# Causal mask of a second attention: from mask products on TensorE to selects on GpSimd

## The reference

```python
h = _rms(x, n1_w)                       # x: 4 x 256 x 128
q = _rms(heads(wq), qn_w); k = _rms(heads(wk), kn_w); v = heads(wv)   # 16 heads of width 8
scores = jnp.einsum('bhqd,bhkd->bhqk', q, k) * HD ** (-0.5)
causal = jnp.tril(jnp.ones((T, T), bool))
scores = jnp.where(causal[None, None], scores, -jnp.inf)
attn = jax.nn.softmax(scores, axis=-1)
ao = jnp.einsum('bhqk,bhkd->bhqd', attn, v).transpose(0, 2, 1, 3).reshape(B, T, C) @ wo.T
ao = ao.at[:, :, :M].set(0.0)           # M = 32
x = x + ao
xf = _rms(x, n2_w).reshape(-1, C)       # then four experts with top-2 gating
```

## Time and profile before

| | |
|---|---|
| three runs | 288.17, 284.63, 287.77 us; median 287.77 |
| the profiled execution | 285.92 us; its span 284.2 us |
| granted TensorE clock, mean | 0.971 |
| PE, DVE, ACT, POOL busy | 77%, 57%, 45%, 26% of the span |

### The profile page before, as it was taken

How to read it: one execution, slowest core, us unless ns; L and a number is a source line. 1 busy time by engine, 2 the same in 40 slices (tenths; PEclk the granted TensorE clock), 3 DMA queues, 4 the chain that set the end, 5 groups by cost and what they waited for, 6 DMA issues and landing times.

```text
span 284.2 us, 4855 instructions
## 1 busy us (share of the span) xinstructions
PE 219.1 (77%) x1906; PEld 150.6 (53%) x1906; DVE 160.8 (57%) x335; ACT 128.5 (45%) x175; POOL 74.1 (26%) x77
## 2 busy tenths in 40 slices
PE   0387987788988899885924697878985997788983
PEld 0244454424444644642724484556663885777973
DVE  1888699372552682582474878858515145842313
ACT  0206695882744254250350427976576340524230
POOL 4516589910005026039006022000003011000000
PEclk9999999999999999997995899999999999999997
DMA  6800090000052060150060000000000000000000
GB/s 199 374 1 0 7 287 11 0 1 2 0 128 42 25 145 0 41 127 2 18 144 7 0 0 2 0 2 0 1 2 0 2 0 0 1 21 18 0 18 18
DMA packets 10067, 11.73 MB, mean 41 GB/s; under 512 B 928, under 2 KB 9648, under 8 KB 9792
## 3 DMA queue, kind: packets, MB, share of 16 engines
q1 hardware_dynamic: 10048, 11.47, 14.3%
HBM read 10.38 MB, written 1.09 MB: 40 GB/s over the span
## 4 chain that ended last, share of the span: by engine, by line
PE 53%; DVE 25%; ACT 11%; POOL 4%; issue 4%; DMA 2%; POOLq 0%; DVEq 0%; SPq 0%; ACTq 0%
PE banks L1516 11%; PE banks L1272 8%; PE banks L1239 5%; DVE probs L888 5%; PE banks L1300 4%; PE banks L1551 3%; PE banks L1167 3%; PE banks L1421 3%; PE banks L1371 2%; ACT probs L546 2%; PE banks L1292 2%; DMA rows<-in_rows 2%; PE banks L1399 2%; PE banks L1322 2%; ACT probs L585 2%
## 5 line engine op out<-in xcount | busy, mean ns | idle before, releaser
L888 DVE TENSOR_TENSOR probs<-probs,eb 128x1024 f32<-128x1024 f32 x24 | 29.7, 1251 | 31.9 <-ACT probs L546 31.9
L585 ACT ACTIVATE probs<-banks,shift 128x1024 f32<-128x1024 f32 x24 | 26.4, 1116 | 24.6 <-PE banks L1403 24.6
L1272 PE MATMUL banks<-probs,kvt 128*64 128x512 f32 (+1 forms) x128 | 24.9, 522 | 8.5 <-DVE probs L888 8.3
L546 ACT ACTIVATE probs<-banks,key_shift 128x1024 f32<-128x1024 f32 x24 | 25.9, 1112 | 12.0 <-PE banks L1239 11.5
L1239 PE MATMUL banks<-qt,kT 64*128 64x512 f32 x96 | 25.3, 628 | 2.6 <-ACT probs L546 2.1
L360 POOL TENSOR_TENSOR qin<-qss,minus_half 128x16 f32<-128x16 f32 x8 | 23.1, 2904 | 7.9 <-DVE qss L727 7.7
L1272 PEld LDWEIGHTS banks<-probs,kvt 128*64 128x64 f32 x128 | 8.2, 144 | 22.1 <-DVE probs L888 12.2
L1371 PE MATMUL banks<-ident_bf,parts 128*128 128x128 bf16 x128 | 10.1, 242 | 11.8 <-DVE parts L961 9.3
L1117 DVE SCALAR_TENSOR_TENSOR x<-banks,ga,x 128x96 f32 (+1 forms) x32 | 10.2, 318 | 15.4 <-PE banks L1551 11.4
L1167 PE MATMUL banks<-wa,on 128*128 128x512 f32 x32 | 17.3, 667 | 1.2 <-DVE spread L733 1.2
L389 POOL TENSOR_TENSOR o_raw<-o_raw,spread 128x2048 f32<-128x2048 f32 x2 | 9.1, 4540 | 30.4 <-DMA spread<-softmax_inverse_sums 30.4
(11 more groups left out here) (214 smaller groups left out, 442.3 us busy)
## 6 DMA issues: line engine op xcount, KB each, us to landing
spread<-softmax_inverse_sums SPq DMA_DIRECT2D x16, 256.0 KB, 5.9
eb<-bias_table SPq DMA_DIRECT2D x4, 512.0 KB, 6.2
wb<-in_wb SPq DMA_DIRECT2D x1, 1842.0 KB, 10.9
wa<-in_wa SPq DMA_DIRECT2D x1, 1160.0 KB, 7.4
x<-in_x SPq DMA_DIRECT2D x1, 512.0 KB, 4.1
softmax_inverse_sums<-zin SPq DMA_DIRECT2D x4, 128.0 KB, 1.7
out<-x SPq DMA_DIRECT2D x4, 128.0 KB, 1.8
rows<-in_rows SPq DMA_DIRECT2D x1, 456.0 KB, 6.0
```

What stands on the lines that cost most here:

```text
L546: nc_.activation(pb[c], sc[:, 1024 * (c % 2):1024 * (c % 2 + 1)], ACT.Exp, bias=key_shift[:, b, k:k + 1]).then_inc(s["exp_done"], 1)
L585: nc_.activation(pb[c], sc[:, 1024 * SLOT[c]:1024 * (SLOT[c] + 1)], ACT.Exp, bias=shift2[:, 3:4]).then_inc(s["exp2_done"], 1)
L888: v.tensor_tensor(p, p, w, ALU.mult).then_inc(s["mult_done"], 1)
L1272: last = mm(out, vn[:, b, part], rhs, start=(part == 0), stop=(part == 2))
```

## The change

The tiles `later` and `later_bf` go, with the POOL instructions that build them, and the 48 mask products (two in each of 24 chunks). Each score product now stands alone in its region of PSUM. POOL gets an `affine_select` for each chunk, which writes zeros over the exponentials of later keys, in place: four blocks of 128 columns for chunks with k < 2 (512 elements in a partition), eight for k = 2 (1024). Each waits for the chunk's exponential. `values2` waits for the selects of its group instead of for the exponentials. POOL's order in the first batch is written out: selects 0 to 2 ahead of `rstd_of_y(2)`, select 3 behind it, selects 4 and 5 between `rstd_of_y(3)` and `group_rstd(2)`. For the later batches POOL's hardware loop becomes a Python loop, with the copy into `v2f` and then the six selects; the roots of the second norm come behind the last of them.

```diff
--- before.py
+++ after.py
@@ -109,7 +109,6 @@
 
         ident = sb("ident", [P, P])
         sum_rows = sb("sum_rows", [P, 4, 32])
-        later = sb("later", [P, P])
         minus_half = sb("minus_half", [P, H])
         ln_eps = sb("ln_eps", [P, B * T])
         rms_eps = sb("rms_eps", [P, 4])
@@ -192,7 +191,6 @@
         rest = sb("rest", [P, 3, T * H, HD])
         v2 = qt[:, 0].rearrange("p m i -> p (m i)")[:, B * S:2 * B * S].rearrange("p (b t h d) -> p b t h d", b=B, t=T, h=H)
         ident_bf = sb("ident_bf", [P, P], BF16)
-        later_bf = sb("later_bf", [P, P], BF16)
         gain2 = sb("gain2", [P, HD])
         v2f = sb("v2f", [P, T, H, 32])
         o2s = keys_space[:, B * S:B * S + 1024].rearrange("p (g c) -> p g c", g=2)
@@ -239,7 +237,7 @@
             zmax_done zinv_ready zinv_stored zinv_spread on_ready y_done y_parts y_stat y_var y_rstd y_norm x2_done
             r_stat r_var r_rstd h2_ready h2_turned hT2_ready qkv_done raw_ready sq2_ready s64_ready r64_ready qkn_ready
             v2_done sq_x_ready p3_dve
-            v2f_ready operands_zeroed part_done parts_ready parts_turned operands2_ready qk2_chunk exp2_done pv2_done o2_evac o2_turned ao_ready ao_turned
+            v2f_ready operands_zeroed part_done parts_ready parts_turned operands2_ready qk2_chunk exp2_done later_zeroed pv2_done o2_evac o2_turned ao_ready ao_turned
             aoT_ready wo_done x3_done p4_dve
             f_stat f_var f_rstd f_ready f_turned xfT_ready gate_done lg_ready gate_w xs_ready gates
             gate_exp res_part u_done u_act silu_a h1_ready down_done stored""".split()
@@ -332,7 +330,7 @@
 
             pool.iota(pos[:], pattern=[[P, T]], base=0, channel_multiplier=1,
                       allow_small_or_imprecise_dtypes=True).then_inc(s["pos_ready"], 1)
-            for buf, value in ((minus_half, -0.5), (ln_eps, 1e-5), (ident, 0.0), (later, 0.0), (sum_rows, 0.0),
+            for buf, value in ((minus_half, -0.5), (ln_eps, 1e-5), (ident, 0.0), (sum_rows, 0.0),
                                (tri, 1.0), (rms_eps, EPS * D)):
                 pool.memset(buf[:], value)
             pool.memset(xk[:, :, P - 1:P], 0.0)
@@ -340,8 +338,6 @@
             step(pool.memset(kvs[:, :, KEYS:XS], 0.0))
             pool.affine_select(out=ident[:], in_=ident[:], compare_op=ALU.not_equal, fill=1.0, base=0,
                                pattern=[[-1, P]], channel_multiplier=1)
-            pool.affine_select(out=later[:], in_=later[:], compare_op=ALU.is_ge, fill=-FAR, base=0,
-                               pattern=[[1, P]], channel_multiplier=-1)
             for k in range(4):
                 pool.memset(sum_rows[:, k, k:k + 1], 1.0)
             pool.affine_select(out=tri[:], in_=tri[:], compare_op=ALU.is_ge, fill=0.0, base=-1,
@@ -392,7 +388,6 @@
                 rstd(mv[:, :, 1], ln_eps, ve[:], rs[:], s["y_stat"], s["y_rstd"], s["y_var"], b)
 
             pool.tensor_copy(ident_bf[:], ident[:])
-            pool.tensor_copy(later_bf[:], later[:])
             pool.memset(v2f[:], 0.0)
             pool.memset(parts[:], 0.0).then_inc(s["sums_cleared"], 1)
             normalised(0)
@@ -408,6 +403,13 @@
                 pool.wait_ge(s["pv2_done"], 2 * b)
                 pool.tensor_copy(v2f[:, :, :, 0:HD], v2[:, b]).then_inc(s["v2f_ready"], 1)
 
+            def later_zeros(b, c):
+                pool.wait_ge(s["exp2_done"], 6 * b + c + 1)
+                n = 4 if c % 3 < 2 else 8
+                block = pb[c].rearrange("p (n i) -> p n i", n=n)[:, :, 0:P]
+                pool.affine_select(out=block, in_=block, compare_op=ALU.is_ge, fill=0.0, base=0,
+                                   pattern=[[0, n], [1, P]], channel_multiplier=-1).then_inc(s["later_zeroed"], 1)
+
             group_rstd(0)
 
             pool.wait_ge(s["qk_chunk"], 6 * (B - 1))
@@ -416,13 +418,20 @@
             normalised(B - 1)
             pool.wait_ge(s["v2_done"], 1)
             values2_in_place(0)
+            for c in range(3):
+                later_zeros(0, c)
             rstd_of_y(B - 2)
+            later_zeros(0, 3)
             group_rstd(1)
             rstd_of_y(B - 1)
+            later_zeros(0, 4)
+            later_zeros(0, 5)
             group_rstd(2)
             pool.wait_ge(s["v2_done"], 3)
-            with pool.Fori(1, B) as b:
+            for b in range(1, B):
                 values2_in_place(b)
+                for c in range(6):
+                    later_zeros(b, c)
 
 
             for h in range(2):
@@ -1396,16 +1405,11 @@
                         lhs, rhs = kT2[:, e, m, 0:P], qT2[:, m]
                     else:
                         lhs, rhs = kT2[:, e, m, P:S], qT2[:, m, P:S]
-                    mm(sc[:, at + wide * i:at + wide * (i + 1)], lhs, rhs, start=(i % (n // 2) == 0), stop=False, skip_group_check=True)
-
-                for j in range(2):
-                    bank = halves(sc[:, at + 512 * j:at + 512 * (j + 1)], n // 2)
-                    last = mm(bank[:, :, 0:P], ident_bf[:], later_bf[:, None, :].to_broadcast([P, n // 2, P]), start=False, stop=True,
-                              skip_group_check=True)
+                    last = mm(sc[:, at + wide * i:at + wide * (i + 1)], lhs, rhs, start=True, stop=True)
                 last.then_inc(s["qk2_chunk"], 1)
 
             def values2(b, g):
-                pe.wait_ge(s["exp2_done"], 6 * b + 3 * g + 3)
+                pe.wait_ge(s["later_zeroed"], 6 * b + 3 * g + 3)
                 pe.wait_ge(s["v2f_ready"], b + 1)
                 pe.wait_ge(s["p4_dve"], 1)
                 if not (isinstance(b, int) and b == 0):
```

## The result

The changed kernel takes 298.7 us (median of five, 295.3 to 301.1) against 287.8 us (median of five, 284.5 to 288.2 and one of 563.9): the ratio is 1.037, with a 95% interval of 1.031 to 1.044. I had forecast 290.9, with 297.0 as the upper end. The profiled execution took 298.68 us, its span 297.0 us, 12.8 us more than before.

A forecast was written before the change was run, and what follows sets the result against it. It took the kernel as mostly PE-bound (53% of the chain). The walk's +2.5 us and 0.6 for DVE's company made +3.1: 285.92 became 289.0, plus 1.85 to the runs' median gave 290.9 us, range 286.5 to 297.0.

The forecast's parts named there:

- walk of waits: Second attention, batch by batch to the second norm's roots: select waits less mask gains, +2.5 us.
- the 0.6 that I had added: Addition to the walk: four of six selects run beside DVE's copies or splits, 0.15 us more each.
- DVE's company: POOL is slower beside DVE: 0.15 us more on four of six selects, +0.6 us in all.
- Rival 2: PE's clock halves in the last batch's idle gaps, slowing gate and first expert's products: up to 2 us, 292.9; chance 0.10.
- the 3.92 us of the earlier trace: Idle time before 131.07 us, after which the granted clock stood at half; each new single gap is shorter.
- The 2.9 us: Most that removing the mask products can give: eleven places on the chain, nine short pairs and two long.
- three signs: Prediction wrong if select's mean is over 1.5 or under 0.5 us, first batch comes later, or last batch's clock falls.
- upper end of 297.0: Top of the forecast range for the whole kernel, set to take in most of rival 1.
- rival 1: Six selects on the path run at the two-operand rate, 2.27 us each: 9.9 us slower, 297.7 us; chance 0.17.
- the select's price: POOL's select costs what a copy would: 1.04 us for eight blocks, about 0.61 us for four.
- POOL's order: First norm's root not delayed by selects; second norm's roots queue behind the last select and start 2.53 us later.

The follow-up runs named there:

- e2: Neither mask products nor selects, against the kernel before; values wait for the exponentials: 290.2 us, ratio 1.010.
- e1: Changed kernel with the 48 mask products put back, selects and the values' wait for them kept: 296.3 us, 1.035 times the kernel before.
- e3: Kernel before's mask products kept; POOL runs same-shaped selects on a spare stretch and values don't wait for them: 292.8 to 298.1 us over four runs.
- e4: Changed kernel with four or eight identity products on PE ahead of each wait for the selects: 298.2 us, 1.041 times the kernel before.
- e7: Changed kernel with batch 0 masked by products on PE, batches 1 to 3 by POOL's selects: 292.4 us, 1.021 times the kernel before.

## Why the prediction was wrong

*The walk of waits was right.* Distances between the landmarks of my walk, before, forecast and measured, in us; (1,0) is the values product of batch 1, group 0, and the last column takes off what the values product between them took over 1.51 us:

| from, to | before | forecast change | measured change | less slow values |
|---|---|---|---|---|
| values (1,0) to (1,1) | 4.90 | +0.88 | +2.43 | +1.15 |
| (1,1) to (2,0) | 7.29 | -0.61 | -0.70 | -0.70 |
| (2,0) to (2,1) | 4.90 | +0.89 | +1.01 | +1.01 |
| (2,1) to (3,0) | 6.71 | -0.03 | +1.29 | +0.23 |
| (3,0) to the roots | 4.41 | +1.40 | +1.41 | +1.41 |
| sum | 28.21 | +2.53 | +5.44 | +3.10 |

(Starts before: 187.67, 192.57, 199.86, 204.76, 211.47 and 215.88; after: 191.66, 198.99, 205.58, 211.49, 219.49, 225.31. Values (1,0) took 2.79 us, (2,1) 2.57. The starts before are the chain's, by which I had walked; the timeline has 187.60, 199.79 and 211.40 for three of them, and by it the sums are +5.37 and +3.03.) The waits came to 3.1 us, my 2.5 and the 0.6 that I had added; that this 0.6 was DVE's company is not borne out, since the six selects on the path took 1.09 us each with DVE beside some of them. That the roots stand behind the last select was right.

*Rival 2 was the step that failed, in its chance and in its price.* I gave the clock 0.10 and up to 2 us, in one place, the last batch, wrote against it that each single gap is shorter than the 3.92 us of the earlier trace rows, and forecast everything behind the gate at its old length. The runs show that this was no bound. In the changed kernel PE finished its scores of the first batch at 158.80 and the mean of the microsecond from 160 to 161 was already 0.79:

```profile
160.00:161.00 1.00, 0.00 (x0) 0.00 (x0) 1.00 (x3) 0.51 (x1) 0.78 (x2) 0.79 0.00 0
...
161.00:162.00 1.00, 0.00 (x0) 0.00 (x0) 1.00 (x1) 0.00 (x0) 0.91 (x1) 0.50 0.00 0
```

The row PEclk of the page shows how often it came: six separate groups of slices under 9, where before there were two and the last slice. Its price in this profile: about 3 us of PE's work in the first stretch (transposes, values, one projection at 2.4 us instead of 1.53), 2.3 us in the two values products of the table, and 3.0 us after the gate: some 8.3 of 12.8 us. With 3.1 for the waits, 1.8 for DVE (below) and 1.1 less at the start, 0.7 us are left. About 0.4 of it lies between the roots and the gate (3.63 us, 3.23 before), which waited for the last values at half clock; the rest is the wait for a select ahead of the values at 191.66 (0.56 us), where my walk had the select and the mask's gain cancel. In whole runs: the kernel before itself took 285.0 us at a mean clock of 0.970 and 287.4 at 0.952, and without selects or products (e2) it went to 290.2 at 0.935. I had also looked only at the wait that the change adds. e2 has no new wait and loses 1%, at lower levels of the clock in eight of ten runs: there the mask products were work that kept the clock up, at no cost on most of the path. They are not all of it: e1 and e3 have all of them, and their clock is 0.938 and 0.937. The 2.9 us that I set as the most their removal can give was right as a bound and said nothing about the loss.

The Trainium skill (TensorE: Matmul & The Clock Gate, Part 1), which I had named for this rival, says that the gate looks at recent activity. e2's levels and e4's last batch, whose values behind their filler take 1.51 us instead of 2.79, agree with it. I used it for one place and one gap.

*The price of DVE's company was put on the wrong engine.* This is the second step that failed. I charged POOL 0.15 us for running beside DVE. What happened is that DVE ran slower beside POOL: 5.15 us for a split of 3.37, shown by e3 (no wait, same length) and e7 (no select, 3.38). The row was there: beside the slowed copy of the earlier trace rows, at 194.30, the kernel before has a slowed cast of DVE, and I read the pair for POOL alone:

```profile
159.12 0.55 DVE L947 CAST parts<-qt 128x768 bf16<-128x768 f32 x1
...
194.55 0.76 DVE L947 CAST parts<-qt 128x768 bf16<-128x768 f32 x1
```

In the first batch I had walked only POOL's queue, which did hold (the root at 163.82 waited for DVE, not for a select), and not the engine beside it, which PE waits for. This is +1.8 us. It isn't what made the clock fall there: the fall came at about 160.6, and an undisturbed split would have ended at 161.1.

*My signs and my range.* Two of the three signs that I had named for a wrong prediction came: the first batch came out later (its values at 165.59, against 163.85, although its split began 1.1 us earlier), and the clock fell in the last batch; the gate came 9.8 us later than 219.1, not 2.5 to 3. That two runs, 295.3 and 295.8 us, fall under my upper end of 297.0 is luck: that end was put there for most of rival 1, which is false, and whose own price of 297.7 lies above it.

*What stays right:* the select's price, POOL's order, the masks' 1.6 us from batch 1 to the gate at full clock (e2), and rival 1 being false.

*What stays open:* why the clock falls in the experts in some executions of one kernel and not in others. The kernel before shows both (0.970 and 0.952), and no experiment here could choose between them. How the clock's part divides between e2's cause (products gone) and the new waits is open too, and the parts don't add: e1 puts the products back, and its ratio is 1.035 against 1.037. What the rows show is what the lower clock cost where it came, not what each fall was owed to.

## What to carry to other kernels

Before work is taken off the matrix engine, look at what else keeps it busy there: where it already waits for others, products beside those waits may cost nothing and hold the clock, and removing them can cost more than they took. Moving an elementwise step to POOL has three prices, its latency on the path, what queues behind it on POOL, and what it does to DVE beside it (here 3.37 us of DVE's work became 5.15); read DVE's own chain for the last. List every kernel's runs with their mean clock before comparing two medians.

## What was not expected of the hardware

- A granted clock that falls to half after less than 2 us without work (158.80 to about 160.6), when PE had worked little before too: 1.2 GHz and transposes of 1.07 us at 1.89 us.
- One kernel's runs fall on few levels: the kernel before at 0.970 or 0.976, 0.952, 0.949 and 0.941 with about 285, 287.4, 288.3 and 289.8 us.
- A cast of DVE, f32 to bf16 in SBUF, of 0.42 us takes 1.31 us beside a 1024-element select of POOL, while the select itself goes from 1.09 to 1.34. The cast ends 0.28 us after the select.
